# Last stage of a graph layer: the low halves of each quad in two subtractions instead of four, and the layer norm's scaling moved to ScalarE

## What is computed

```
d  = 1 / sqrt(sum(A, axis=-1))
z  = leaky_relu((d * (A @ (d * x))) @ W1 + b1)            # first Laplacian product
S  = exp(-distance(z_i, z_j) / 2), only the 4 nearest kept per row
A2 = S + A
d2 = 1 / sqrt(sum(A2, axis=-1))
out = layernorm(x + (d2 * (A2 @ (d2 * x))) @ W2 + b2)     # second Laplacian product
```

## Time and profile before

| | |
|---|---|
| median of 3 runs | 2786.36 us (2783.97 to 2786.53) |
| profiled execution, span from its first to its last instruction | 2783.8 us, clock 0.973 |
| busy: PE, DVE, ACT, POOL | 90%, 85%, 55%, 40% of the span |
| last stage's stretch of halved rows (u = 34 to 127) | 2436 to 2767 us, 331 us |
| last two plain quads and the last finish | 2767 to 2784 us |

### The profile page before, as it was taken

How to read it: one execution, slowest core, us unless ns; L and a number is a source line. 1 busy time by engine, 2 the same in 40 slices (tenths; PEclk the granted TensorE clock), 3 DMA queues, 4 the chain that set the end, 5 groups by cost and what they waited for, 6 DMA issues and landing times.

```text
span 2783.8 us, 29281 instructions
## 1 busy us (share of the span) xinstructions
PE 2510.5 (90%) x9468; PEld 1742.1 (63%) x9468; DVE 2367.3 (85%) x1666; ACT 1526.7 (55%) x1765; POOL 1118.3 (40%) x937
## 2 busy tenths in 40 slices
PE   1377999999999998889999999999999997998998
PEld 0133444444577776557878787878778775466665
DVE  7988898977678887999999998998998786399997
ACT  0000000000366776778888888878888774166664
POOL 0000000000000000017778778787878895566660
PEclk9788999999999999999999999999999998999999
DMA  9998999995789870005455555555455569999995
GB/s 385 421 394 370 385 420 421 421 414 214 269 326 347 331 297 31 0 1 167 151 156 155 155 148 157 153 159 146 133 173 147 174 205 402 367 366 359 357 357 220
DMA packets 144638, 713.46 MB, mean 256 GB/s; under 512 B 18625, under 2 KB 26561, under 8 KB 82561
## 3 DMA queue, kind: packets, MB, share of 16 engines
q1 hardware_dynamic: 123072, 669.71, 64.6%
q0 software_dynamic: 16832, 33.84, 5.0%
q10 hardware_dynamic: 4608, 8.39, 0.8%
HBM read 679.62 MB, written 32.24 MB: 256 GB/s over the span
## 4 chain that ended last, share of the span: by engine, by line
PE 60%; DVE 13%; DMA 10%; issue 8%; ACT 4%; POOL 2%; SPq 1%; POOLq 0%; ACTq 0%; DVEq 0%
PE PS L602 16%; PE PS L696 5%; PE PS L697 5%; PE PS L698 5%; DMA cache<-at 5%; DVE al_t L1396 4%; PE PS L787 4%; PE PS L731 3%; PE PS L732 3%; DMA ring<-at 3%; PE PS L741 3%; DVE R L1350 3%; PE PS L662 3%; PE PS L700 2%; PE PS L656 2%
## 5 line engine op out<-in xcount | busy, mean ns | idle before, releaser
L1074 POOL TENSOR_TENSOR al<-ring,ah 128x1024 fp32r<-128x1024 f32 x252 | 608.4, 2415 | 201.0 <-ACT ah L917 191.1
L1350 DVE MAX8 R<-R 128x8 f32<-128x8192 f32 x64 | 555.9, 8686 | 94.0 <-ACT R L946 93.3
L946 ACT ACTIVATE R<-PS 128x1024 f32<-128x1024 f32 x512 | 517.5, 1019 | 187.3 <-PE PS L700 107.7
L1353 DVE FIND_INDEX8 R<-R,R 128x8 uint32<-128x8192 f32 x64 | 555.8, 8685 | 0.0
L1047 POOL CAST zst<-zh 128x128 fp32r<-128x128 f32 (+1 forms) x64 | 23.7, 370 | 1205.0 <-DVE zl L1302 879.6
L696 PE MATMUL PS<-zh,zst 128*128 128x512 f32 x1024 | 411.3, 402 | 30.2 <-ACT PS L932 23.5
L697 PE MATMUL PS<-zl,zst 128*128 128x512 f32 x1024 | 402.8, 393 | 0.0
L698 PE MATMUL PS<-zh,zst 128*128 128x512 f32 x1024 | 402.0, 393 | 0.0
L602 PE MATMUL PS<-cache,R 128*128 128x512 f32 x680 | 307.7, 607 | 31.2 <-DVE R L1248 16.3
L932 ACT ACTIVATE PS<-R 128x1024 f32<-128x1024 f32 x315 | 323.1, 1026 | 6.9
L1205 POOL DMA_INDIRECT R<-xs_dram,R x256 | 256.2, 1001 | 128.9 <-issue 72.8
(11 more groups left out here) (165 smaller groups left out, 4265.8 us busy)
## 6 DMA issues: line engine op xcount, KB each, us to landing
R<-at SPq DMA_DIRECT2D x151, 1024.0 KB, 8.6
ring<-at SPq DMA_DIRECT2D x144, 1024.0 KB, 6.9
ring<-at SPq DMA_DIRECT2D x252, 512.0 KB, 3.8
cache<-at SPq DMA_DIRECT2D x125, 1024.0 KB, 18.7
raw_sq<-at SPq DMA_DIRECT2D x22, 1024.0 KB, 7.5
raw_z<-at SPq DMA_DIRECT2D x21, 1024.0 KB
raw_ring<-at SPq DMA_DIRECT2D x21, 1024.0 KB, 8.6
acc_dram<-R POOLq DMA_DIRECT2D x63, 256.0 KB, 5.7
```

The lines of the kernel that those rows point to most:

```text
L946: act.activation(score[j % 2][:, c * EC:(c + 1) * EC].rearrange("p (b c) -> p b c", b=2), pair(first, j, c), ACT.Copy).then_inc(copied, 1)
L1074: pool.tensor_tensor(al[:, k % SPLIT], raw[k % RAW], ah[:, k % SPLIT].bitcast(F32), ALU.subtract)\
L1350: v.max(top[:, j], score[j % 2]).then_inc(dve3, 1)
L1353: v.max_index(place[:, j], top[:, j], score[j % 2]).then_inc(placed, 1)
```

## The change

`rest_t` makes the low halves in two instructions of 128 x 1024, each of which raises `al_dve` (`RESTS = 2`); PE waits for the first before its first two `al_t` matmuls and for the second before the last two; SP, which waits for the buffer to be read, waits for the second.

`normalize` goes from DVE at F+6 to ACT at F+8, ahead of `store`. DVE keeps the reciprocal and adds one instruction on 128 x 4 numbers, `shift = -mean * rstd` (`scale_and_shift`), which raises `shift_ok`; ACT then does `rstd * xb + shift` in four activations of 128 x 128 (`Identity`, scale and bias taken from `small`) and raises `out_ok`, for which its own `store` waits.

```
-        def wait_rest(eng, u):
+        def wait_rest(eng, u, part_=RESTS - 1):
             if place_of[u] < BY_POOL:
                 eng.wait_ge(al_pool, place_of[u] + 1)
             else:
-                eng.wait_ge(al_dve, place_of[u] - BY_POOL + 1)
+                eng.wait_ge(al_dve, RESTS * (place_of[u] - BY_POOL) + part_ + 1)
...
-                wait_rest(pe, u)
                 for k in range(TB):
+                    if k % (TB // RESTS) == 0:
+                        wait_rest(pe, u, k * RESTS // TB)
                     i = pe.matmul(bank, xsh[:, h * TB + k], al_t[n % 2][:, k], start=False, stop=False)
...
+            def normalize(f):
+                act.wait_ge(shift_ok, f + 1)
+                if f >= 2:
+                    act.wait_ge(s_out[f % 2], 16 * (f // 2))
+                for j in range(TB):
+                    i = act.activation(res[f % 2][:, j], xb[f % 2][:, j], ACT.Identity,
+                                       bias=shift[f % 2][:, j:j + 1], scale=rstd[f % 2][:, j:j + 1])
+                i.then_inc(out_ok, 1)
...
                     if u == FIN_AT[f] + 8:
+                        normalize(f)
                         store(f)
...
-                for k in range(TB):
-                    i = v.tensor_tensor(al_t[n % 2][:, k], raw_t[u % RAW_T][:, k], ah_t[n % 2][:, k].bitcast(F32),
-                                        ALU.subtract)
-                i.then_inc(al_dve, 1)
+                for part_ in range(RESTS):
+                    ks = slice(part_ * TB // RESTS, (part_ + 1) * TB // RESTS)
+                    v.tensor_tensor(al_t[n % 2][:, ks], raw_t[u % RAW_T][:, ks], ah_t[n % 2][:, ks].bitcast(F32),
+                                    ALU.subtract).then_inc(al_dve, 1)
...
-            def normalize(f):
+            def scale_and_shift(f):
                 v.wait_ge(std_ok, f + 1)
                 lt(v.reciprocal(rstd[f % 2], rstd[f % 2]))
-                if f >= 2:
-                    v.wait_ge(s_out[f % 2], 16 * (f // 2))
-                for j in range(TB):
-                    i = v.tensor_scalar(res[f % 2][:, j], xb[f % 2][:, j], mv[f % 2][:, j, 0:1],
-                                        rstd[f % 2][:, j:j + 1], ALU.subtract, ALU.mult)
-                i.then_inc(out_ok, 1)
+                v.scalar_tensor_tensor(shift[f % 2], mv[f % 2][:, :, 0], -1.0, rstd[f % 2], ALU.mult, ALU.mult)\
+                 .then_inc(shift_ok, 1)
```

More of the change, by code:

```diff
@@ L35 @@
 BY_POOL = 2
+RESTS = 2
 LIGHTS, HEAVIES = range(HB), range(HB, B)
@@ L272, in build @@
         res = [cut1(BC).rearrange("p (j d) -> p j d", j=TB) for _ in range(2)]
-        small = sb("small", [P, 2 * TB * (6 + 2 + 1)])
+        small = sb("small", [P, 2 * TB * (6 + 2 + 1 + 1)])
         ct = [0]
@@ L282, in build @@
         rstd = [cut2(TB) for _ in range(2)]
+        shift = [cut2(TB) for _ in range(2)]
         PS = ctx.enter_context(nc.psum_tensor("PS", [P, 8, BC], F32))
@@ L368, in build @@
         std_ok = sem("std_ok")
+        shift_ok = sem("shift_ok")
         out_ok = sem("out_ok")
@@ L1034, in _ @@
             root_var(B - 1)
+            normalize(B - 1)
             store(B - 1)
@@ L1476, in _ @@
                     if u == FIN_AT[f] + 6:
-                        normalize(f)
+                        scale_and_shift(f)
             add_bias(B - 1)
@@ L1480, in _ @@
             moments(B - 1)
-            normalize(B - 1)
+            scale_and_shift(B - 1)
 def kernel(x, adj, L0_gnn_W1, L0_gnn_b1, L0_gnn_W2, L0_gnn_b2):
```

## The result

| | before | with the change |
|---|---|---|
| median of 10 runs each | 2786.1 us (2783.97 to 2791.62) | 2779.95 us (2776.34 to 2785.52) |
| ratio of with to before | | 0.9977, 95% interval 0.9968 to 0.9986 |
| span of the profiled execution | 2783.8 us | 2778.2 us |
| its clock | 0.973 | 0.972 |

What follows compares the result with a forecast made beforehand. Bound: a two-buffer ring of DVE, PE and ACT in the last stage, DVE having most work. 2.0 + 1.9 + 8.3 + 0.7 + 2.8 - 1.4 - 0.5 = 13.8 us saved, predicting 2773 us, range 2764 to 2782.

Steps and rivals of the forecast that it cites:

- the half that comes earlier: After a rest, `prod_t` comes 0.46 us earlier: 2.8 us gained at entries to plain pairs, 2.4 at six `heavy_y`.
- The normalisation on ACT: At F+8, before the rounding of F+9: takes 1.4 us on ACT, 7 x 0.2 = 1.4 us lost.
- well over 0.39 us: Sign of being wrong: activations with two operands, in the normalisation on ACT, taking well over 0.39 us.
- elsewhere ACT's waits for PE hide the four: Outside the seven finishes charged 0.2 us, ACT's waits for PE, 1.6 us each, hide the four normalisation activations.
- It plays no part: From 2436 to 2767 us the granted clock is 1.00, its upper level, so it has no effect.
- Two instructions take 2.36 us: Each rest on DVE takes 2.36 us in two instructions instead of 2.50 in four, saving 0.14 per quad.
- DVE's shorter rests: Halved quads: 0.14 us of DVE time saved per rest, 59 x 0.14 = 8.3 us at the other rests.
- The step at F+6: From rest F+6 to F+7, ACT's rounding limits: 0.25 us saved at eight finishes (2.0), some 0.95 at two (1.9).
- DVE's waits for ACT grew and PE's for DVE shrank: Sign of being right: in the last stage DVE's waits for ACT grow from 19.1 us, PE's for DVE shrink.
- That loads do not end last: Last stage: loads have 8.8 us to spare; the rival that they take the gain (2780 or 2786 us) had chance 0.15.
- The end: Last finish, without cover: a small operation more and a hand-over to ACT, 0.5 us lost.
- all of DVE's time comes out: Rival, last stage: all DVE time saved reaches the end, 24 us, giving 2762 us; chance 0.10.

Runs made afterwards that it cites:

- f2: Kernel before with only the rests in two subtractions of 1024, two increments and PE's two waits; 2775.97 us, ratio 0.9964.
- f3: Kernel before with only the normalisation moved to ACT at F+8, rests left as four of 512; 2790.3 us, ratio 1.0016.
- g4: Whole change with activations that take only the scale, leaving out the shift; 2773.22 us, ratio 0.995.
- f4: Whole change with the store at F+9 instead of F+8; 2772.37 us, ratio 0.9951.
- g3: Kernel before with rests in two subtractions of 1024 but one increment and one PE wait; 2777.21 us, ratio 0.9965.
- h1: Whole change with only finish 14's store moved from F+8 to F+9; 2778.65 us, ratio 0.9972.
- g1: Whole change with the store at F+9 and `weigh` ahead of the other small steps of its quad; 2768.66 us, ratio 0.9929.
- h3: Whole change with `weigh` first, normalisation at F+9 and store at F+10; 2771.16 us, ratio 0.9948.
- f1: The whole change run again, unaltered, beside its parts on one chip; 2781.38 us, ratio 0.9984 to the kernel before.
- h2: Whole change with normalisation and store both at F+9; 2781.18 us, ratio 0.998.
- e2: Kernel before with only the normalisation moved to ACT at F+8, on a chip where before takes 2876.58 us; 2869.29 us, ratio 0.9977.

## Why the prediction was wrong

**By parts.** The forecast was 13.8 us, of which 0.5 lost at the very end, behind the last reciprocal, so 14.3 by the ruler; 6.6 were found. Of the 14.3, the rests alone were to bring 13.2: 69 x 0.14 = 9.7, less 1.7 at the `heavy_y`, and 2.4 + 2.8 for the half that comes earlier. They brought 10.3 (f2). The normalisation on ACT was to add the remaining 1.1, and took away 3.7 (f2 to the whole change; 3.1 alone, in f3). Two steps failed.

**The step that failed first is the normalisation on ACT: its cost, and the overlap that was to hide it.** I put it at 1.4 us and counted 7 x 0.2 = 1.4 us of loss. It holds ACT for 2.06: 1.64 for four activations with two per-row operands, and 0.43 for the store's wait. An activation takes 0.48 us, which the prediction itself had named as a sign of being wrong ("well over 0.39 us"). Both parts were in reach. The second operand's price stood in the text as a sentence beside the sum, with 3 us for it; it is 5.1 (g4). The store's wait I had as 0.14 on top of 1.26; it is 0.43 in which everything behind stands still, and 6.9 us in all (f4). And "elsewhere ACT's waits for PE hide the four" did not hold: by my own count 0.66 us more at seven finishes would be 4.6, but they come out at nearly all fourteen: up to finish 14, g4 and f4 bring 3.6 + 5.2 = 8.8 us of the 4.9 + 5.6 = 10.5 that they take off ACT. That the four stand in front of the rounding of F+9, for which DVE waits, was right.

**The second step that failed is the half that comes earlier.** It was put at 2.8 + 2.4 = 5.2 us; f2 less g3 is 0.8 by the ruler (1.1 up to finish 10). Before u = 48 PE is the later one already (its last low halves at 2481.74 take 1.08 us without a wait), so `prod_t` is no earlier there; before u = 80 and u = 96 it does wait, 0.68 and 0.58 us. And f2 waits for the gathers more than g3 does, 14.2 against 5.9 us. How the miss divides between the two is not settled.

**The clock.** "It plays no part" held for the kernel before and not for the one with the change: a PE wait of 2.00 us near 2751 ends in half speed, which with the wait that brings it about costs 1.6 us (h1).

**What held.** Two instructions take 2.36 us. DVE's shorter rests: 9.7 - 1.7 = 8.0 forecast, and g3 has 9.5 by the ruler. The step at F+6: 3.34 us instead of 3.65, and a DVE that waits there, as foreseen (0.25 taken, 0.31 found at finish 1). DVE's waits for ACT grew and PE's for DVE shrank. ACT's four with one operand take 1.26. That loads do not end last: ACT's waits for them are gone from the list of 2436 to 2767. The end costs 0.75 us (from the last reciprocal to the end of the span 3.82 before, 4.57 after) where I had 0.5.

**Misread, with little harm.** `neighbours` stands on F+6 at three finishes and not at two: at finish 6 too, where the step shrinks from 4.31 to 3.34 us. And at f = 8 and 13 the quad behind F+6 is not plain; they stand behind a plain pair, two quads on. PE sets the time there either way: the steps, 5.94 and 5.98 us before, shrink by 0.13 and 0.18. Over the ten finishes that I gave 3.9 us the steps shrink by 5.3.

**What does not add up.** The two costs on ACT, each taken away alone, are worth 5.1 + 6.9 = 12.0 by the ruler. In both the fall of the clock behind finish 14 is gone, so 1.4 of it is counted twice, and 10.6 is left (if the two add up, which no run shows). With neither cost the normalisation would then have brought 10.6 - 3.7 = 6.9 us, where the forecast, its own 1.4 of loss put back, had 2.5. So more of the time freed on DVE comes out, once ACT lets it, than I had allowed, by some 4 us; the 1.4 us at F+6 are a part, and which finishes give the rest I did not trace. The rival "all of DVE's time comes out" was the farthest off, but it is what g1 comes near (19.6 of 24.4), once ACT's order is mended. That the forecast missed by no more than 7.7 us is thus in part luck: the cost on ACT was too small by much, and DVE's gain too small as well.

**A version that beats both kernels** is g1: the change, the store one quad later, and `weigh` ahead of the other small steps. 2768.66 us beside 2787.36, ratio 0.9929.

## What to carry to other kernels

When work moves from the busiest engine to one in the same ring, cost it on the receiver as that engine runs it: with its per-row operands, and with the time in which its queue stands still for a wait on its own last result. Put an instruction that waits for the engine's own output behind the next piece of independent work (each of them: in h3 the store had moved, and a load took its place), and put work that is ready ahead of work that waits for another engine; here the two turned a gain of 6.6 us into 19.6 without removing anything.

## What the runs showed of the hardware that I had not expected

- A DMA issue on ACT that waits for ACT's own last activation leaves the engine idle for 0.43 us before the next activation (all of the 10 rows with `weigh` behind it; 0.48, 0.48 and 0.76 us before a `heavy_y`), 0.35 of it the issue. Without such a wait, in f4, the issue at 2462.72 runs while `weigh` is at work, and nothing is lost.
- One PE wait of 2.00 us was followed by some 4 us at the lower clock, and so were 2.02 (f1) and 2.00 (h2) near the same place; in h1, f4 and g4 the wait at the same place was 1.48, 1.49 and 1.65 us, and the clock stayed up. Length alone does not decide it: PE's longest wait for a rounding, 2.18 us before 2683.60 in the trace of the whole change, was followed by matmuls at the upper level, 0.23 us apart.
- The same program takes 2786 us on some chips and 2877 or 2891 on two others; on the first of these two (e2) a load was rounded 28 us after its issue, the other has no trace of an unchanged kernel. A difference of 0.2% can't be measured there, and a change that looks like 2.4% there (the shorter rests) is 0.36% elsewhere.
